# Masking by zeroing exponentials on GpSimdE in place of mask matmuls on TensorE

## The reference

```
x = x + 0.5 * ffn(layernorm(x))          # 128 -> 384 -> 128, silu(gate) * up, integer weights / 127
x = x + attn(layernorm(x))               # 4 query heads, 2 key/value heads, 32 features each
x = x + 0.5 * ffn(layernorm(x))

# attn(x): h = rmsnorm(x) * w;  q, k = l2norm of h Wq, h Wk;  v = h Wv
s = einsum('bhqd,bhkd->bhqk', q, k) * exp(log_temperature)
s = where(causal, s, -inf)
out = softmax(s) @ v;   return x + gate * (out @ Wo)
```

## Time and profile before

| | us |
|---|---|
| median of the runs | 483.7 |
| the profiled execution's own time | 483.82 |
| span of its trace | 482.0 |
| TensorE busy in the span | 415.5 (86%) |
| VectorE busy | 351.1 (73%) |
| ScalarE busy | 387.7 (80%) |
| GpSimdE busy | 265.7 (55%) |
| GB/s moved by the DMA queues, mean | 72 |

### The profile page before, as it was taken

How to read it: one execution, slowest core, us unless ns; L and a number is a source line. 1 busy time by engine, 2 the same in 40 slices (tenths; PEclk the granted TensorE clock), 3 DMA queues, 4 the chain that set the end, 5 groups by cost and what they waited for, 6 DMA issues and landing times.

```text
span 482.0 us, 10470 instructions
## 1 busy us (share of the span) xinstructions
PE 415.5 (86%) x3734; PEld 214.4 (44%) x3734; DVE 351.1 (73%) x847; ACT 387.7 (80%) x553; POOL 265.7 (55%) x332
## 2 busy tenths in 40 slices
PE   0678997881787999999999999999999997899995
PEld 0345654570242443543534434524534344565664
DVE  5788887658649686968868869868763908887653
ACT  4699996672587798898897897988987997999962
POOL 5398999653553443535354263453030373999953
PEclk9999999996889999999999999999999999999999
DMA  5575322412320906307206106025052022454542
GB/s 152 131 145 141 66 44 44 67 22 67 67 44 0 175 2 132 46 2 133 44 0 142 32 16 151 9 66 111 1 73 60 2 45 44 89 116 103 131 110 71
DMA packets 119131, 34.89 MB, mean 72 GB/s; under 512 B 101552, under 2 KB 119088, under 8 KB 119088
## 3 DMA queue, kind: packets, MB, share of 16 engines
q1 hardware_dynamic: 118080, 34.15, 34.6%
q10 hardware_dynamic: 1008, 0.20, 0.2%
HBM read 4.98 MB, written 4.19 MB: 19 GB/s over the span
## 4 chain that ended last, share of the span: by engine, by line
PE 53%; DVE 14%; issue 12%; POOL 9%; ACT 8%; DMA 2%; POOLq 1%; DVEq 1%; ACTq 0%; SPq 0%
PE ps L444 11%; PE ps L624 10%; PE ps L605 9%; PE ps L629 9%; PE ps L491 4%; PE ps L482 4%; ACT PT L719 2%; PE ps L513 2%; DVE X L902 2%; DVE H L304 2%; POOL HL L369 2%; POOL RMS L819 2%; DVE AN L892 2%; PE ps L651 2%; POOL rv L815 2%
## 5 line engine op out<-in xcount | busy, mean ns | idle before, releaser
L719 ACT ACTIVATE PT<-ps,k_exp 128x1024 f32<-128x1024 f32 (+1 forms) x192 | 162.5, 901 | 22.6 <-PE ps L609 17.9
L605 PE MATMUL ps<-QKT 128*128 128x512 f16 (+3 forms) x384 | 88.7, 333 | 24.3 <-ACT PT L719 13.8
L444 PE MATMUL ps<-XT,WT 128*128 128x512 f16 x384 | 95.5, 387 | 15.9 <-ACT SG L411 7.5
L624 PE MATMUL ps<-PT,V 128*32 128x512 f32 (+3 forms) x768 | 82.0, 499 | 1.3 <-ACT PVS L753 1.3
L629 PE MATMUL ps<-PT,ones 128*32 128x512 f32 (+3 forms) x768 | 79.9, 487 | 0.0
L369 POOL TENSOR_TENSOR HL<-H,HH 128x1024 f16<-128x1024 f32 x32 | 68.2, 2131 | 17.8 <-ACT HH L415 17.8
L304 DVE SCALAR_TENSOR_TENSOR H<-SG,k_isilu,ps 128x1536 f32<-128x1536 f32 x32 | 57.9, 1809 | 14.1 <-ACT SG L411 9.9
L258 POOL TENSOR_TENSOR OL<-ON,OH 128x512 f16<-128x512 f32 x16 | 19.5, 1217 | 81.9 <-ACT OH L254 81.9
L605 PEld LDWEIGHTS ps<-QKT 128*128 128x128 f16 x384 | 28.1, 98 | 81.5 <-ACT PT L719 62.7
L444 PEld LDWEIGHTS ps<-XT,WT 128*128 128x128 f16 x384 | 34.1, 99 | 64.1 <-issue 18.8
L393 ACT ACTIVATE XN<-X,NB,RS 128x128 f32<-128x128 f32 x128 | 52.4, 483 | 3.3 <-POOL NB L347 3.3
(11 more groups left out here) (120 smaller groups left out, 639.7 us busy)
## 6 DMA issues: line engine op xcount, KB each, us to landing
result<-X SPq DMA_DIRECT2D x16, 256.0 KB, 2.5
X<-in_L_attn_x SPq DMA_DIRECT2D x7, 512.0 KB, 4.8
X<-in_L_attn_x SPq DMA_DIRECT2D x2, 256.0 KB, 4.9
XT<-w_int SPq DMA_TRANSPOSE x32, 3.1
AXT<-AS SPq DMA_TRANSPOSE x16, 3.1
QKT<-ST SPq DMA_TRANSPOSE x16, 4.7
w_int<-in_L_ffn_w_gate SPq DMA_DIRECT2D x1, 192.0 KB, 4.1
w_int<-in_L_ffn_w_up SPq DMA_DIRECT2D x1, 192.0 KB, 4.4
```

Of the source, the lines that this page charges most:

```text
L444: i = e.matmul(out[:, j, :], WT[:, wp, w * NJ + j, :], XT[k % 2][:, xp, :], start=a == 0, stop=a == len(passes) - 1)
L605: i_ = e.matmul(o, QKT[k % 2][:, i // TPC, NH + hp, i % TPC * P:(i % TPC + 1) * P], QKT[k % 2][:, qc, 2 * hp + h, CH - n:CH], start=True, ...
L624: e.matmul(PVD[HD * h:HD * h + HD, 0, CH - n:CH], V[k % 2][:, i, v0:v0 + HD], PT[g % 2][:, h, 0:n], start=i == 0, stop=done, skip_group_ch ...
L719: e.activation(PT[g % 2][:, 2 * hp:2 * hp + 2, 0:n], SCORES[hp][:, :, 0:n], ACT.Exp, scale=k_exp[:, 0:1]).then_inc(a_exp, 1)
```

## The change

The mask matmuls of line 609 are left out of the version that runs (`diag` is now true only with `shift`). In their place GpSimdE goes over the exponentials: for each diagonal group and head pair one `affine_select` on the 128 masked columns of two heads, in place in `PT`, which writes zero where the query comes before the key. A new semaphore `a_msk` counts these, and each head's matmul of line 624 in a diagonal group waits for its pair. GpSimdE's loop over the batches is now written out in full, and its attention program stands twice, behind the flag. There are 128 selects in place of 256 matmuls.

```diff
-                diag = i >= TPC * qc
+                diag = shift and i >= TPC * qc
...
                 for h in range(NH):
+                    if g in DIAG and not shift:
+                        e.wait_ge(a_msk, 2 * (b * len(DIAG) + DIAG.index(g)) + h // 2 + 1)
                     v0 = DQ + DK + HD * (h // 2)
...
+            def mask(b, g):
+
+                if shift:
+                    return
+                for hp in range(2):
+                    e.wait_ge(a_exp, 2 * (b * NG + g) + hp + 1)
+                    p = PT[g % 2][:, 2 * hp:2 * hp + 2, 0:P]
+                    e.affine_select(out=p, in_=p, compare_op=ALU.is_ge, fill=0.0, base=0,
+                                    pattern=[[0, 2], [1, P]], channel_multiplier=-1).then_inc(a_msk, 1)
...
             stack_lo(1, 1)
+            mask(0, 0)
             rstds(2, 0)
+            mask(0, 1)
             rstds(3, 1)
             x_lo(2, 0)
             x_lo(3, 1)
...
+                if k >= 1:
+                    mask(b, 1)
                 if later:
                     rstds(m0 + 2, 0)
+                mask(b, 2)
+                mask(b, 3)
                 if k >= 1:
                     o_lo(e, b * 2 - 1)
...
                     stack_lo(m0 + 1, 1)
+                mask(b, 8)
+                mask(b, 9)
                 o_lo(e, b * 2)
+                mask(b, 10)
                 if later:
                     x_lo(m0 + 2, 0)
+                mask(b, 11)
+                if later:
                     x_lo(m0 + 3, 1)
...
+                else:
+                    mask(b + 1, 0)
+            for k in range(B):
+                step(k, k)
...
+            hot = is_hot(e)
+            by_heat(e, att_pool, hot, lambda: ffn_pool(e, 1))
```

More of the change, by code:

```diff
@@ L169, in macaron_kernel @@
             "full", "free", "cp", "s", "exp", "pv", "pvc", "rd", "on", "oh", "ol", "mx", "last")]
+        a_msk = sem("a_msk")
         d_f, d_x, d_t, d_u = [[sem(f"{n}{i}") for i in range(2)] for n in ("d_f", "d_x", "d_t", "d_u")]
@@ L523, in macaron_kernel @@
         G0 = TPC
+        DIAG = [g for g, (qc, i) in enumerate(groups) if i >= TPC * qc]
         USES = {0: [("qkv", 0, 0), ("qkv", 0, 1)], 1: [("qkv", 1, 0), ("qkv", 1, 1)],
@@ L798, in att_act, with att_pool @@
             pv_out(B * 2 - 1, B * NG)
-        def att_pool(e, first=None):
+        def att_pool(e, shift, first=None):
             def rstds(m, half):
@@ L867, in step @@
                     ffn_pool(e, 1, [("x_hi", 2), ("x_lo", 2), ("rstd", 4)])
-            drive(e, step, B, 1, 3)
+                else:
+                    mask(b + 1, 0)
+            for k in range(B):
+                step(k, k)
         def att_dve(e, shift, first=None):
@@ L1157, in _ @@
             ffn_pool(e, 0, None, {-1: down_weights,
[L1158 to L1165, removed]
+                                  8: lambda: att_pool(e, False, ("rstds_a", 0)),
+                                  9: lambda: att_pool(e, False, ("rstds_b", 0)),
+                                  10: lambda: att_pool(e, False, ("rstds_a", 1)),
+                                  11: lambda: att_pool(e, False, ("rstds_b", 1)),
+                                  12: lambda: att_pool(e, False, ("x_lo", 0)),
+                                  13: lambda: att_pool(e, False, ("x_lo", 1))})
+            hot = is_hot(e)
+            by_heat(e, att_pool, hot, lambda: ffn_pool(e, 1))
         @block.scalar
```

## The result

| kernel | median, us | against before (95%) | first batch | a steady batch |
|---|---|---|---|---|
| before | 483.8 | | 41.78 | 33.99 |
| changed | 494.7 | 1.022 (1.018 to 1.026) | 51.84 | 34.08 |
| changed, again | 494.2 | 1.022 (1.019 to 1.025) | 52.09 | 34.04 |
| e1_first | 487.2 | 1.007 (1.005 to 1.008) | 45.19 | 34.05 |
| x_nomask | 478.6 | 0.989 (0.987 to 0.991) | 41.02 | 33.37 |

The last two columns come from the one profiled execution of each kernel: from the start of the first weigh of a batch to that of the next, the third batch standing for the steady ones. The changed kernel is slower by 10.9 us.

What follows compares the result with a forecast made beforehand. PE was taken to set the pace, though not everywhere, with waits for exponentials and `OL`. First batch +8.2, steady batches +0.6, last batch -0.3 sum to +8.5 us on 483.82: 492.3 us, range 486 to 498.5 (8 times in 10).

Steps and rivals of the forecast that it cites:

- its own mechanism: First-batch select order delays PE while steady batches lose almost nothing: 489 to 494 us, chance 0.43.
- the rival in which the port decides: Selects of groups 9 and 10 delay VectorE, then exponentials of group 11: 0.4 us a batch, 495 us, chance 0.2.
- The gate of the first batch: Selects of groups 2 and 3 queue behind GpSimdE's third coefficient block: weigh of group 2 starts 12.4 us later.
- The end of the first batch: Net first-batch delay: +9.0 us through the projections, groups 8 to 11 give back 0.8, so +8.2 us.
- Steady batches: Groups 0 to 3 keep 0.2 us, group 10's select behind `OL` costs 0.3: +0.1 us each, +0.6 for six.
- The last batch: Groups 0 to 3 keep some saving, groups 8 to 11 meet second-layer preparation on GpSimdE: -0.3 us.
- The select: Time of one new GpSimdE select over two heads: 0.43 us taken, bounds 0.29 to 0.59 us.
- the rival of the slow select: Each select takes 0.59 us, about 1 us more a steady batch: 499.8 us, chance 0.15.
- Costed at nothing: Flag load, branch, per-head waits (0 to 3 us in all); selects of groups 0, 1, 8, 9 0.3 to 1 us early.
- The port: VectorE and GpSimdE share a port: 0.43 us per meeting select; by the skill's rule the sum is about 2 us higher.
- The saving is kept: Six steady batches and the last keep up to 1.84 us each: 479.1 us; chance 0.06 faster, 0.03 no change.

Runs made afterwards that it cites:

- changed, again: The changed kernel run once more with no edit, for a second profile and time: 494.2 us.
- e1_first: Changed kernel with the first batch's selects of groups 2 and 3 moved ahead of the third coefficient block: 487.2 us.
- x_nomask: Changed kernel with no selects and no waits for them, the causal mask inside diagonal blocks left out of the computation: 478.6 us.
- x_fill: Changed kernel plus 92 idle matmuls on TensorE ahead of weigh of group 2 in the first batch: 492.3 us.
- h_no10: e1_first with group 10 alone masked by matmuls again, the other seven diagonal groups by selects: 485.4 us.
- s_89b: Changed kernel with selects in groups 8, 9 and 11 only, mask matmuls in groups 0 to 3 and 10: 482.4 us.
- x_wide: e1_first with selects of groups 0, 1, 2, 8, 9 and 10 over 256 columns a head instead of 128: 493.5 us.
- s_fill3: s_89b plus idle TensorE matmuls in three waits of the first batch (ahead of first scores, scores of groups 4 and 8): 480.6 us.
- x_side: Changed kernel with mask matmuls back; selects run at their places over a scratch tile and TensorE does not wait for them: 486.8 us.
- e2_ol: e1_first with the select of group 10 ahead of `OL` instead of behind it: 489.8 us.

## Why the prediction was right

492.3 us was forecast, 494.2 and 494.7 were measured: inside the stated range, but just above the 489 to 494 that the forecast gave to its own mechanism, and next to the 495 of the rival in which the port decides. The time alone could not tell the two apart; the experiments do, and they show the forecast's mechanism.

- **The gate of the first batch** was right to the tenth: weigh of group 2 was to come 12.4 us later after the first scores and came 12.4 later; scores of group 4 were to be 9.7 us later and were 9.75 (144.93 less 2.27 for the later start, against 132.91). e1_first shows that it is the order.
- **The end of the first batch** is the term that was mis-sized. Up to weigh of group 4 the batch lost 9.3 us (9.0 forecast), of which x_fill shows two as the clock. Then groups 4 to 11 were to give back 0.8 and cost 0.8 instead, because the clock fell once more at 164 us: 4.29 us from weigh of group 7 to that of group 8, 2.83 before. That gives +10.1 instead of +8.2 (10.3 in the second profile), and most of what the forecast missed. That a saving of 0.23 us a group can be taken away by the clock was not in the sum.
- **Steady batches**: +0.1 each was forecast; the six together gave +0.1 and -0.1 in the two profiles. Both halves of the argument hold: groups 0 to 3 bring nothing by selects (33.64 with them in h_no10, 33.54 without in s_89b; the forecast kept 0.2), nor without any mask (x_nomask), and group 10 is a gate worth 0.4 us.
- **The last batch**: -0.3 forecast, -0.1 measured.
- **The select**: 0.43 us taken, 0.415 measured; the rival of the slow select is out, and x_wide shows that its price was about right: 0.2 us more cost 6.2 us over e1_first.
- **Costed at nothing**: the selects of groups 8 and 9 were to come 0.3 to 1 us before weigh needs them. Those of group 8 have 0.2 us to spare in a steady batch of e1_first, and in the first batch of h_no10 and s_fill3 weigh of group 8 waits 0.32 us for one.
- **The port** as a rival is out in the changed kernel: x_side has the selects and keeps its steady batches, and VectorE is busy for 27.82 us of the steady batch with the selects as without them (x_nomask). In x_side VectorE is held up, 1.0 us a batch. The Trainium skill (SBUF — State Buffer, section "SBUF: two separate sides") has a port that the two engines share; the 1.0 us agree with it. The 2 us that the forecast gave for that rule did not arrive. In e2_ol, where `AS` lies beside the update of x, the trace reads as if it counts; that was not tried.
- **The saving is kept**: x_nomask shows that at most 5.1 us of 14.7 could be had, less than the 8.2 that this rival needed.

## What to carry to other kernels

Work that is moved to an engine with room in its busy share takes the place in that engine's queue, and there inherits every wait in front of it: read the queue around each new instruction, in the first pass of a loop above all, where the order is another. Take work off the busiest engine only where it waits for nothing in the same stretch; a run with that work left out prices the most that can be won before anything is moved, here a third. Then move it only in those places where the result comes in time, here three groups of eight.

## What the runs showed of the hardware

The granted clock fell to half again in the first batch at the two waits of scores of group 8 (2.07 and 0.40 us) in six profiles: at the end of the first wait in e1_first, between the two in e2_ol, and 0.3 to 0.9 us after the second in the changed kernel (twice), x_fill and s_89b. After the same two waits it stayed full in x_nomask, x_wide and h_no10; what decides it is open. Where the first of them was filled (s_fill3) it did not fall, and the six times of s_fill3 lie within 0.5 us, the eight of s_89b within 1.4.
